# An edge loop of graph attention on Trainium2: another order of VectorE's work, with the running maximum ahead of the merge

## The chip, the cores and the metric

The kernel runs on one core of one Trainium2 chip, which has eight. The metric is the device time of one execution in microseconds, the median of several. Its engines: TensorE (PE, with its weight loads as PEld), VectorE (DVE), ScalarE (ACT), GpSimd (POOL) and SyncE (SP); the last two here mostly issue transfers, which 16 DMA engines carry out.

## The reference

One layer for 1250 nodes of 512 features and 20000 edges that are sorted by their target node:

```
xn = layernorm(x)
r  = [xn[src], xn[dst], edge] @ Wr.T + br ;  k = r @ Wk.T + bk ;  v = r @ Wv.T + bv      # 8 heads of 64
a  = sum over a head of q[dst] * k, times 1/8
attn = softmax of a over the edges of each target ;  out = segment_sum(v * attn, dst) @ Wo.T + bo
x  = x + batchnorm(xn + out) + linear_attention(xn)
x  = x + ffn(layernorm(x))                        # ternary weights, activations rounded to int8
```

The change is in the part from the edge products to the segment sums.

## The kernel before, in words

A prologue folds the weights, so that an edge's key and value are the edge's features times two 512x512 matrices (M) plus a row of a table of the source node, and writes to HBM a table of queries, a table of keys and values, and four empty tables (merge0 to merge3) of merged rows. Then the function `edges` runs over the 20000 edges, in 157 tiles of 128 edges, two tiles to a pair, 79 pairs. After it come the linear attention, the sums over the tables and the feed-forward part.

Products keep float32 precision by splitting each operand into a high part (rounded to fp32r, made by ScalarE) and a low part (the rest, made by VectorE). For a pair p:

- SyncE loads dst_line and end_line (lines 1099 and 1101, target and run-end indices broadcast to all partitions), cut_line (1105) and the edge features efT (1096, 512 KB a pair). Its queue works in order; dst_line of a pair waits for the one-hots of the pair two before, cut_line for a scan (line 1104), and the next efT is issued behind that.
- GpSimd issues indirect transfers, one for each tile: the queries q (qc), the older merged rows (old) and the keys and values of the source (kv), line 1111, and it stores merged rows into a table (merge<-new, line 1140).
- TensorE: `keys` and `values` (24 matmuls a tile, 128x512, lines 1401 to 1405), `sort_scores` (1428, 1429) brings the scores into an order by runs of equal target, `turn_runs` (1437) transposes their running maximum, `spread_top` (1446, 1447) takes each edge's run maximum to its row, and `sums` (1462 to 1465) adds the exponentials and weighted values of equal targets.
- VectorE: `add_k`, `times_q`, `sum_scores` (1255, 1264, 1273) and `add_v` (1307) use the products; `row_one_hots` (1242, 1246), `rank_one_hots` (1234) make the matrices of the sums; `scan` (1322) is the running maximum; `maximum` (1331, 1336, 1338) takes the maximum with the older row of the target and the differences for the exponential; `exp_low_part` (1298), `wv_low_part` (1314), `runs_low_part` (1290), `low_part` (1227) are low parts; `scale_den` (1346) and `merge_rows` (1355, 1357) add the sums to the older rows.
- ScalarE: `high_part` (1166), `copy_runs` (1173), `weights` (1182 exponential, 1184 its high part), `weigh_v` (1193 eight heads, 1198 high part), `scale_old` (1205).

All engines loop over p from 0 to 80, each with an order written out by hand, and wait for each other's semaphores. Each works in its order alone: an instruction that waits holds up all that stand behind it. In turn p, TensorE makes the keys and values of pair p, the run maxima of pair p - 1 and the sums of pair p - 2; VectorE merges pair p - 2 and takes the maximum of pair p - 1. GpSimd's order in a turn is

```
fetch_q(p + 1) ; fetch_old(p - 1) ; fetch_kv(p + 1) ; store(p - 2)
```

where the store waits for the end of `merge_rows(p - 2)` (line 1136). A fetch of older rows waits for the store of the pair two before into the same table (line 1132), and `maximum` waits for the landing of the fetched rows (line 1328). `sort_scores(p)` on TensorE waits for the merge of pair p - 2 (line 1427).

Of the kernel before, what the change touches and what calls it, by code (L numbers as in the profile page):

```python
# [50 lines left out]
def tiles_of(p):  # L51
    return 2 if 2 * p + 1 < ET else 1
# [932 lines left out]
def edges(nc, ef, q_table, kv_table, merge, ident, Me_hi, Me_lo, dst_rows, end_rows, cut_rows, src_id, dst_id, put_id,  # L985
          dst_f, rank, iota_row, iota_col, xT_hi, xT_lo, xnT):

    with ExitStack() as ctx:
# [54 lines left out]
        def landed(p):  # L1043

            return 16 * sum(tiles_of(k) for k in range(p % 2, p + 1, 2))
# [19 lines left out]
        def newmax_at(p):  # L1065

            return 3 * p + 1

        def diff_at(p):
            return 3 * p + 3  # L1070

        def scaled_at(p):

            return 2 * p + 1
# [4 lines left out]
        def exp_at(p):  # L1079

            return 2 * p + 1

        def exp_hi_at(p):
            return 2 * p + 2
# [74 lines left out]
        @block.scalar  # L1159
        def _(act):  # L1160
            def high_part(p):
                b, n = p % 2, tiles_of(p)
                act.wait_ge(ef_in[b], 16 * (p // 2 + 1))
                if p >= 2:
                    act.wait_ge(v_done, 2 * (p - 1))
                act.activation(efT_hi[b][:, 0:n, :, :], efT[b][:, 0:n, :, :], ACT.Copy).then_inc(hi_ready, 1)  # L1166

            def copy_runs(p):
                n = tiles_of(p)
                act.wait_ge(runs_turned, 2 * p + n)  # L1170
                if p >= 1:
                    act.wait_ge(top_done, 2 * p)
                act.activation(runs_hi[:, 0:n, :], turned_s[:, 0:n, :], ACT.Copy).then_inc(runs_copied, 1)

            def weights(p):
                n = tiles_of(p)
                act.wait_ge(max_step, diff_at(p))
                if p >= 2:
                    act.wait_ge(summed, 2 * (p - 1))
                    act.wait_ge(den_step, scaled_at(p - 2))  # L1180
                    act.wait_ge(exp_low, p - 1)
                act.activation(expd[p % 2][:, 0:n, :, :], diff[p % 2][:, 0:n, :, :], ACT.Exp, scale=SCALE).then_inc(exp_ready, 1)  # L1182
                act.wait_ge(exp_ready, exp_at(p))
                act.activation(exp_hi[p % 2][:, 0:n, :], expd[p % 2][:, 0:n, 0, :], ACT.Copy).then_inc(exp_ready, 1)

            def weigh_v(t):
                p, u = t // 2, t % 2
                act.wait_ge(exp_ready, exp_at(p))
                act.wait_ge(v_added, t + 1)
                if p >= 1:  # L1190
                    act.wait_ge(wv_lo_ready, t - 1)
                for h in range(H):
                    act.activation(wv[:, u, h * DH:(h + 1) * DH], vv[p % 2][:, u, h * DH:(h + 1) * DH], ACT.Copy,  # L1193
                                   scale=expd[p % 2][:, u, 0, h:h + 1]).then_inc(wv_ready, 1)
                act.wait_ge(wv_ready, H * (t + 1))
                if p >= 1:
                    act.wait_ge(summed, t - 1)
                act.activation(wv_hi[:, u, :], wv[:, u, :], ACT.Copy).then_inc(wv_hi_ready, 1)  # L1198

            def scale_old(p):  # L1200
                for u in range(tiles_of(p)):
                    act.wait_ge(old_in[p % 2], landed(p))
                    for h in range(H):
                        rows = old[p % 2][:, u, h * DH:(h + 1) * DH]
                        act.activation(rows, rows, ACT.Copy, scale=expd[p % 2][:, u, 1, h:h + 1]).then_inc(old_scaled, 1)  # L1205

            high_part(0)
            for p in range(PAIRS + 2):
                if p >= 2 and tiles_of(p - 2) == 2:
                    weigh_v(2 * p - 3)  # L1210
                if p + 1 < PAIRS:
                    high_part(p + 1)
                if p >= 2:
                    scale_old(p - 2)
                if 1 <= p <= PAIRS:
                    copy_runs(p - 1)
                    weights(p - 1)
                    weigh_v(2 * p - 2)

        @block.vector  # L1220
        def _(dve):
            def low_part(p):
                b, n = p % 2, tiles_of(p)
                dve.wait_ge(hi_ready, p + 1)
                if p >= 2:
                    dve.wait_ge(v_done, 2 * (p - 1))
                dve.tensor_tensor(efT_lo[b][:, 0:n, :, :], efT[b][:, 0:n, :, :], efT_hi[b][:, 0:n, :, :].bitcast(F32),
                                  ALU.subtract).then_inc(lo_ready, 1)
# [64 lines left out]
            def exp_low_part(p):  # L1293
                b, n = p % 2, tiles_of(p)
                dve.wait_ge(exp_ready, exp_hi_at(p))
                if p >= 2:
                    dve.wait_ge(summed, 2 * (p - 1))
                dve.tensor_tensor(exp_lo[b][:, 0:n, :], expd[b][:, 0:n, 0, :], exp_hi[b][:, 0:n, :].bitcast(F32),
                                  ALU.subtract).then_inc(exp_low, 1)

            def add_v(t):
                p, u = t // 2, t % 2
                dve.wait_ge(v_done, t + 1)
                dve.wait_ge(kv_in[p % 2], landed(p))
                if p >= 2:
                    dve.wait_ge(wv_ready, H * (t - 3))
                dve.tensor_tensor(vv[p % 2][:, u, :], psV[u][:, :], kv[p % 2][:, u, D:2 * D], ALU.add).then_inc(v_added, 1)

            def wv_low_part(t):
                u = t % 2  # L1310
                dve.wait_ge(wv_hi_ready, t + 1)
                if t >= 2:
                    dve.wait_ge(summed, t - 1)
                dve.tensor_tensor(wv_lo[:, u, :], wv[:, u, :], wv_hi[:, u, :].bitcast(F32), ALU.subtract).then_inc(wv_lo_ready, 1)  # L1314
# [10 lines left out]
            def maximum(p):  # L1325
                b, n = p % 2, tiles_of(p)
                dve.wait_ge(top_done, 2 * p + n)
                dve.wait_ge(old_in[b], landed(p))
                if p >= 2:
                    dve.wait_ge(put[b], landed(p - 2))  # L1330
                dve.tensor_tensor(new[b][:, 0:n, ROW:TROW], old[b][:, 0:n, ROW:TROW], top[:, 0:n, :],
                                  ALU.max).then_inc(max_step, 1)
                dve.wait_ge(max_step, newmax_at(p))
                if p >= 2:
                    dve.wait_ge(exp_ready, exp_at(p - 2))
                dve.tensor_tensor(diff[b][:, 0:n, 0, :], score[b][:, 0:n, :], new[b][:, 0:n, ROW:TROW],
                                  ALU.subtract).then_inc(max_step, 1)
                dve.tensor_tensor(diff[b][:, 0:n, 1, :], old[b][:, 0:n, ROW:TROW], new[b][:, 0:n, ROW:TROW],  # L1338
                                  ALU.subtract).then_inc(max_step, 1)
# [22 lines left out]
            for p in range(PAIRS + 2):  # L1362
                here, last, older = p < PAIRS, 1 <= p <= PAIRS, p >= 2
                if last:
                    add_v(2 * p - 2)
                if older:
                    exp_low_part(p - 2)
                    wv_low_part(2 * p - 4)
                if last and tiles_of(p - 1) == 2:
                    add_v(2 * p - 1)  # L1370
                if last:
                    row_one_hots(p - 1)
                    scan(p - 1)
                if older and tiles_of(p - 2) == 2:
                    wv_low_part(2 * p - 3)
                if here:
                    for t in range(2 * p, 2 * p + tiles_of(p)):
                        add_k(t)
                        times_q(t)
                        sum_scores(t)  # L1380
                if last:
                    runs_low_part(p - 1)
                if here:
                    split_scores(p)
                    rank_one_hots(p)
                if p + 1 < PAIRS:
                    low_part(p + 1)
                if older:
                    scale_den(p - 2)
                    merge_rows(p - 2)  # L1390
                if last:
                    maximum(p - 1)
            for c in range(C):
                dve.tensor_tensor(xnT[:, c, :], xT_hi[:, c, :].bitcast(F32), xT_lo[:, c, :].bitcast(F32), ALU.add)

# [450 lines left out]
```

## Time and profile before

| | us |
|---|---|
| median of 3 runs | 1852.33 |
| lowest and highest | 1850.69, 1859.62 |
| the profiled execution, its own time | 1861.11 |
| its span | 1859.4 |
| busy: TensorE | 1625.0 (87%) |
| busy: VectorE | 1301.8 (70%) |
| busy: ScalarE | 1026.1 (55%) |
| busy: GpSimd | 698.6 (38%) |
| first and last sort_scores seen in the edge loop | 296.86, 1405.44 |

The span is from the first to the last instruction that the profile records; the run's own time has 1.7 us more. The edge loop takes some 1110 us of it, about 280 us of prologue stand before it and 450 us of other stages behind it. The granted clock of TensorE was 0.938 of full speed over the span, and 1.00 in the windows of the edge loop from 300 to 1300 us. Times in rows are microseconds from the span's start, and a busy time can overlap another on TensorE, whose matmuls are pipelined. A line number is that of the kernel printed above.

### The profile page before, as it was taken

The numbers are of one execution on the slowest core, as the hardware profiler recorded it, in microseconds if no ns is written. First come the engines' busy times: TensorE is split into PE (matmuls) and PEld (weight loads), VectorE is DVE, ScalarE is ACT, GpSimd is POOL, SyncE is SP. The second block draws the span as 40 slices with busy tenths as digits, with TensorE's granted clock in tenths as the row PEclk, the third lists the DMA queues.
The fourth block names the chain that finished last, engine by engine and source line by source line (L and its number), as shares of the span: only waits on it lengthen the run. The fifth ranks groups of instructions, "written<-read, shape, count | busy, mean of one in ns | idle before, by whom it ended". The sixth has DMA issues, their size and how long they took to land. (4 is left out here: it accounts for less than half of the span.)

```text
span 1859.4 us, 26827 instructions
## 1 busy us (share of the span) xinstructions
PE 1625.0 (87%) x7160; PEld 1189.9 (64%) x7162; DVE 1301.8 (70%) x3259; ACT 1026.1 (55%) x3674; POOL 698.6 (38%) x723
## 2 busy tenths in 40 slices
PE   7989979999999999999999999999992777888523
PEld 6867767777777777777777777777772333444311
DVE  5875728788877888778878788788774445332688
ACT  3982225777677776777677776777664334200011
POOL 0001224555555555555555555555542000000033
PEclk9989989999999999999999999999996788999855
DMA  5664327566656666566665666566652433000001
GB/s 179 204 224 157 123 87 229 190 203 205 220 196 191 207 209 220 192 198 206 220 207 193 207 211 223 195 208 208 203 181 101 142 102 136 0 1 1 23 12 44
DMA packets 129671, 300.29 MB, mean 162 GB/s; under 512 B 29088, under 2 KB 50727, under 8 KB 129522
## 3 DMA queue, kind: packets, MB, share of 16 engines
q0 software_dynamic: 63600, 180.17, 28.7%
q1 hardware_dynamic: 60738, 107.59, 18.7%
q10 hardware_dynamic: 5184, 10.81, 1.5%
q8 instruction: 61, 1.00, 0.2%
q14 instruction: 88, 0.72, 0.1%
HBM read 271.40 MB, written 66.58 MB: 182 GB/s over the span
## 5 line engine op out<-in xcount | busy, mean ns | idle before, releaser
L1193 ACT ACTIVATE wv<-vv,expd 128x64 f32<-128x64 f32 x1256 | 315.2, 333 | 0.0
L1205 ACT ACTIVATE old<-old,expd 128x64 f32<-128x64 f32 x1256 | 307.8, 333 | 0.0
L1140 POOL DMA_INDIRECT merge<-new,put_id x157 | 159.9, 1019 | 374.5 <-DVE new L1357 341.3
L1401 PE MATMUL psK<-M_hi,efT_hi 128*128 128x512 f32 x628 | 253.2, 403 | 6.3 <-ACT efT_hi L1166 6.3
L1401 PE MATMUL psV<-M_hi,efT_hi 128*128 128x512 f32 x628 | 255.8, 407 | 0.0
L1402 PE MATMUL psK<-M_lo,efT_hi 128*128 128x512 f32 x628 | 249.5, 397 | 0.0
L1402 PE MATMUL psV<-M_lo,efT_hi 128*128 128x512 f32 x628 | 249.5, 397 | 0.0
L1314 DVE TENSOR_TENSOR wv_lo<-wv,wv_hi 128x512 fp32r<-128x512 f32 x157 | 108.9, 693 | 196.2 <-ACT wv_hi L1198 190.5
L1111 POOL DMA_INDIRECT kv<-kv_table,src_id x157 | 164.3, 1047 | 74.9 <-issue 30.8
L1182 ACT ACTIVATE expd<-diff 128x32 f32<-128x32 f32 (+1 forms) x79 | 18.1, 229 | 310.4 <-DVE diff L1338 310.4
L1111 POOL DMA_INDIRECT qc<-q_table,dst_id x157 | 155.4, 990 | 53.7 <-issue 46.9
L1405 PE MATMUL psK<-M_hi,efT_lo 128*128 128x512 f32 x628 | 172.8, 397 | 0.0
L1405 PE MATMUL psV<-M_hi,efT_lo 128*128 128x512 f32 x628 | 172.4, 396 | 0.0
L1111 POOL DMA_INDIRECT old<-merge,dst_id x157 | 151.4, 965 | 50.5 <-issue 46.7
L1401 PEld LDWEIGHTS psK<-M_hi,efT_hi 128*128 128x128 f32 x628 | 118.6, 189 | 31.5 <-ACT efT_hi L1166 6.7
L1405 PEld LDWEIGHTS psK<-M_hi,efT_lo 128*128 128x128 f32 x628 | 118.4, 189 | 28.9
L1405 PEld LDWEIGHTS psV<-M_hi,efT_lo 128*128 128x128 f32 x628 | 118.3, 188 | 29.0
L1402 PEld LDWEIGHTS psK<-M_lo,efT_hi 128*128 128x128 f32 x628 | 118.9, 189 | 25.9
L1402 PEld LDWEIGHTS psV<-M_lo,efT_hi 128*128 128x128 f32 x628 | 118.9, 189 | 25.5
L1401 PEld LDWEIGHTS psV<-M_hi,efT_hi 128*128 128x128 f32 x628 | 118.7, 189 | 24.9
L1636 POOL MEMSET onem<- 128x128 f32 x1 | 0.2, 204 | 324.2 <-POOLq L1487 324.2
L1264 DVE TENSOR_TENSOR kq<-kk,qc 128x520 f32<-128x520 f32 x157 | 110.1, 701 | 8.1 <-DMA qc<-q_table,dst_id 2.7
(271 smaller groups left out, 3310.1 us busy)
## 6 DMA issues: line engine op xcount, KB each, us to landing
efT<-in_ef_turned_dram SPq DMA_DIRECT2D x78, 512.0 KB, 6.7
merge<-empty ACTq DMA_DIRECT2D x4, 2640.0 KB, 9.7
rows<-merge SPq DMA_DIRECT2D x40, 264.0 KB, 3.5
row_block<-dst_rows POOLq DMA_DIRECT2D x13, 768.0 KB, 5.9
dst_line<-dst_rows SPq DMA_DIRECT2D x78, 128.0 KB, 3.5
end_line<-end_rows SPq DMA_DIRECT2D x78, 128.0 KB, 5.3
kv_table<-kv_out SPq DMA_DIRECT2D x10, 512.0 KB, 3.3
raw<-in_L_gnn_Wr_dram SPq DMA_DIRECT2D x12, 256.0 KB, 5.4
```

Of the source, the lines that this page charges most:

```text
L1111: pool.indirect_dma_start(out=out, out_offset=None, in_=table[:, :], in_offset=bass.IndirectOffsetOnAxis(ap=ids[:, t:t + 1], axis=0)).then ...
L1140: pool.indirect_dma_start(out=merge[2 * (p % 2) + u][:, :], out_offset=bass.IndirectOffsetOnAxis(ap=put_id[:, t:t + 1], axis=0), in_=new[p ...
L1182: act.activation(expd[p % 2][:, 0:n, :, :], diff[p % 2][:, 0:n, :, :], ACT.Exp, scale=SCALE).then_inc(exp_ready, 1)
L1193: act.activation(wv[:, u, h * DH:(h + 1) * DH], vv[p % 2][:, u, h * DH:(h + 1) * DH], ACT.Copy, scale=expd[p % 2][:, u, 0, h:h + 1]).then_ ...
L1205: act.activation(rows, rows, ACT.Copy, scale=expd[p % 2][:, u, 1, h:h + 1]).then_inc(old_scaled, 1)
L1264: dve.tensor_tensor(kq[:, u, :, :].rearrange("p h e -> p (h e)"), kk[:, u, :, :].rearrange("p h e -> p (h e)"), qc[p % 2][:, u, :], ALU.mu ...
L1314: dve.tensor_tensor(wv_lo[:, u, :], wv[:, u, :], wv_hi[:, u, :].bitcast(F32), ALU.subtract).then_inc(wv_lo_ready, 1)
L1401: pe.matmul(out[:, :], efT_hi[b][:, u, c, :], Me_hi[:, c, col:col + D], start=c == 0, stop=False)
L1402: pe.matmul(out[:, :], efT_hi[b][:, u, c, :], Me_lo[:, c, col:col + D], start=False, stop=False)
L1405: last = pe.matmul(out[:, :], efT_lo[b][:, u, c, :], Me_hi[:, c, col:col + D], start=False, stop=c == C - 1)
L1636: pool.memset(onem[:, :], 1.0).then_inc(cst, 1)
```

## The change

Three moves in VectorE's loop and one in ScalarE's; no operation is added or removed.

- `exp_low_part(p - 2)` and both `wv_low_part` of pair p - 2 now stand behind `row_one_hots(p - 1)` and `scan(p - 1)`; before, the first of them stood between the two `add_v` and the second behind the scan.
- `maximum(p - 1)` now stands ahead of `scale_den(p - 2)` and `merge_rows(p - 2)`; before, behind them.
- The exponentials' high part (line 1184) becomes `weights_high`, issued behind the first `weigh_v` of the pair instead of ahead of it.

```diff
@@ ScalarE
                 act.activation(expd[p % 2][:, 0:n, :, :], diff[p % 2][:, 0:n, :, :], ACT.Exp, scale=SCALE).then_inc(exp_ready, 1)
+
+            def weights_high(p):
+                n = tiles_of(p)
                 act.wait_ge(exp_ready, exp_at(p))
                 act.activation(exp_hi[p % 2][:, 0:n, :], expd[p % 2][:, 0:n, 0, :], ACT.Copy).then_inc(exp_ready, 1)
...
                     weights(p - 1)
                     weigh_v(2 * p - 2)
+                    weights_high(p - 1)
@@ VectorE
                 if last:
                     add_v(2 * p - 2)
-                if older:
-                    exp_low_part(p - 2)
-                    wv_low_part(2 * p - 4)
                 if last and tiles_of(p - 1) == 2:
                     add_v(2 * p - 1)
                 if last:
                     row_one_hots(p - 1)
                     scan(p - 1)
-                if older and tiles_of(p - 2) == 2:
-                    wv_low_part(2 * p - 3)
+                if older:
+                    exp_low_part(p - 2)
+                    for t in range(2 * p - 4, 2 * p - 4 + tiles_of(p - 2)):
+                        wv_low_part(t)
                 if here:
                     for t in range(2 * p, 2 * p + tiles_of(p)):
                         add_k(t)
...
                 if p + 1 < PAIRS:
                     low_part(p + 1)
+                if last:
+                    maximum(p - 1)
                 if older:
                     scale_den(p - 2)
                     merge_rows(p - 2)
-                if last:
-                    maximum(p - 1)
```

## Rows read from the trace of the kernel before

**Rows 1.** Stretch, busy us (instructions) of PE, PEld, DVE, ACT, POOL; granted clock, DMA share, GB/s.
```profile
400.00:1300.00 900.00, 876.17 (x4125) 680.55 (x4123) 723.25 (x1626) 650.53 (x2382) 503.86 (x502) 1.00 0.63 206
```

**Rows 2.** Instructions on the older rows' tile, 400 to 1300 us: starts; issue to landing.
```profile
L1331 DVE TENSOR_TENSOR new<-old,psT x62: 153/167/173, 410.4 to 1288.9; 128x16 f32<-128x16 f32 x62
...
DMA to landing us min/median/max: 5.2/6.6/8.8
```

**Rows 3.** TensorE's order in time, early in the loop: start, duration, line.
```profile
296.86 0.22 PE L1428 MATMUL psO<-to_rank,score_hi 128*8 128x128 f32 x1
...
310.59 0.22 PE L1428 MATMUL psO<-to_rank,score_hi 128*8 128x128 f32 x1
```

**Rows 4.** TensorE's order in time in a steady turn.
```profile
822.15 0.28 PE L1437 MATMUL psT<-ident,runs 8*128 8x8 f32 x2
...
825.73 1.09 PE L1405 MATMUL psV<-M_hi,efT_lo 128*128 128x512 f32 x4
827.05 0.24 PE L1446 MATMUL psT<-runs_hi,from_end 128*128 128x8 f32 x1 [0.23 <-issue]
```

**Rows 5.** VectorE's order in time, the same turn; idle time before in brackets.
```profile
801.56 0.17 DVE L1331 TENSOR_TENSOR new<-old,psT 128x16 f32<-128x16 f32 x1 [1.37 <-issue]
...
814.42 0.17 DVE L1346 TENSOR_TENSOR old_den<-old,expd 128x16 f32<-128x16 f32 x1
...
815.70 0.16 DVE L1357 TENSOR_TENSOR new<-psO,old_den 128x16 f32<-128x16 f32 x1
815.78 0.16 DVE L1331 TENSOR_TENSOR new<-old,psT 128x16 f32<-128x16 f32 x1
...
816.15 0.68 DVE L1307 TENSOR_TENSOR vv<-psV,kv 128x512 f32<-128x512 f32 x1
...
819.36 0.69 DVE L1314 TENSOR_TENSOR wv_lo<-wv,wv_hi 128x512 fp32r<-128x512 f32 x1 [2.40 <-ACT wv_hi L1198]
...
821.19 0.67 DVE L1322 TENSOR_TENSOR_SCAN runs<-cut_line,psO 8x256 f32<-8x256 f32 x1
...
826.77 0.17 DVE L1290 TENSOR_TENSOR runs_lo<-psT,runs_hi 128x16 fp32r<-128x16 f32 x1
...
828.62 0.17 DVE L1346 TENSOR_TENSOR old_den<-old,expd 128x16 f32<-128x16 f32 x1
```

**Rows 6.** ScalarE's order in time in the same turn.
```profile
821.27 0.63 ACT L1198 ACTIVATE wv_hi<-wv 128x512 fp32r<-128x512 f32 x1
...
826.58 0.16 ACT L1173 ACTIVATE runs_hi<-psT 128x16 fp32r<-128x16 f32 x1
```

**Rows 7.** GpSimd's order in time: a store held up, and the steady turn.
```profile
660.19 1.27 POOL L1140 DMA_INDIRECT merge<-new,put_id  x1 [1.99 <-issue]
...
816.68 1.02 POOL L1140 DMA_INDIRECT merge<-new,put_id  x1 [5.76 <-DVE new L1357]
...
823.16 0.95 POOL L1111 DMA_INDIRECT old<-merge,dst_id  x1 [0.30 <-issue]
```

**Rows 8.** SyncE's order in time in the same two turns.
```profile
663.21 0.33 SPq L1096 DMA_DIRECT2D efT<-in_ef_turned_dram  x1
...
822.57 0.33 SPq L1096 DMA_DIRECT2D efT<-in_ef_turned_dram  x1
```

**Rows 9.** Three single second fetches of older rows, each with its landing time.
```profile
L1111 POOL DMA_INDIRECT old<-merge,dst_id x1: 946/946/946, 665.6 to 665.6; - x1
DMA to landing us min/median/max: 5.3/5.3/5.3
...
L1111 POOL DMA_INDIRECT old<-merge,dst_id x1: 944/944/944, 1025.3 to 1025.3; - x1
DMA to landing us min/median/max: 6.0/6.0/6.0
...
L1111 POOL DMA_INDIRECT old<-merge,dst_id x1: 982/982/982, 1399.3 to 1399.3; - x1
DMA to landing us min/median/max: 3.4/3.4/3.4
```

## The prediction, made before the changed kernel was run

> **What bounds the kernel now.** I began with the table by stretches, to see which engine fills the edge loop, where the change is. In its steady part TensorE is busy 876 of 900 us, VectorE 723 and ScalarE 651 [rows 1]: TensorE is the nearest to full, yet it loses 24 us there. One pair of edge tiles is one turn of all the engines' loops; the steady turn is (1288.9 - 410.4) / 61 = 14.40 us, by the 62 maxima of line 1331 [rows 2].
>
> Next, the order in time on TensorE. In the first pairs of the loop, before any merged row holds anyone up, a turn from L1428 to L1428 is 310.59 - 296.86 = 13.73 us [rows 3]. In the steady part the last value product ends its issue at about 825.73 + 4 x 0.234 = 826.67 and spread_top starts at 827.05, 0.38 us late [rows 4]. So TensorE could turn in 13.73, and something else holds it to 14.2 and, in bad turns, to more.
>
> That something is on VectorE and ScalarE. From one maximum (801.56) to the next (815.78), in a turn where the second waited for nothing, is 14.22 us [rows 5]. The chain: differences, exponentials, both weighted values with the second high part ending at 821.27 + 0.63 = 821.90 [rows 6], its low part, keys and scores, runs_lo behind ScalarE's copy of 826.58, low part of the edges, merge, maximum. It holds 2.40 us in which VectorE waits at the first wv_lo, with the scan queued behind it. The maximum at 801.56 had itself waited 1.37 us [rows 5]: for no engine, so for a transfer.
>
> The last view is GpSimd's and the transfers'. The end of a merge (815.70 + 0.16 = 815.86) lets the store go at 816.68; two stores, two fetches of q and two of the older rows follow, the last at 823.16 [rows 5, 7]. The old rows land 5.2 to 8.8 us after their issue, half of them by 6.6 [rows 2]; the second of a pair, which counts, is mostly near 6.8. From merge to landing: 0.82 + 6.48 + 6.8 + 0.1 allowed for the signal = 14.2 us. So a second loop, merge, store, fetch, maximum, is as long as a turn; today it is open, since the maximum stands behind the merge of its iteration and can be late without delaying that store.
>
> **The change, part by part.** No instruction is added or taken away, and no transfer; all is order. M is the start of a maximum, and the rows of 815.78 serve for a turn.
>
> Maximum in front of the merge. The chain through ScalarE loses scale_den and merge, 814.42 to 815.86 = 1.44 us [rows 5]. Its length becomes: wv_hi of the second tile at M+6.12, wv_lo and keys and scores to M+11.0, runs_lo at M+11.1 (ScalarE's copy starts at 826.58 - 815.78 = 10.8), then the 1.85 us to 828.62 with which a merge began before [rows 5, 6]: 13.0 us. That is under 13.73, so this chain ceases to bind. The 0.38 us before spread_top goes, since the copy comes earlier against TensorE's order.
>
> The price: the merge stands 0.37 us later behind the maximum (three small operations, 815.78 to 816.15 [rows 5]), and it is now behind the maximum's wait for the old rows. Queued behind that wait are scale_den, both merges, the store, and behind the store on GpSimd's queue all fetches of q, old rows and kv; TensorE's sort_scores also waits for the merge. The second loop closes: 0.37 + 1.44 + 0.82 + 6.48 + 0.1 + L = 9.2 + L, L being the landing time of the second old fetch. With L = 6.8 it would be 16.0 us a turn; TensorE's 13.73 needs L of 4.5.
>
> Values, one-hots and scan in front of the low parts. Their own length is unchanged, and what was the wait of 2.40 us shrinks, as the second wait for wv_hi falls after the scan. The scan's end was 821.19 + 0.67, M+6.1; it now has the merge of 1.44 us ahead of it, and no longer the wait of 2.40 and the 0.7 us of exp_low and wv_lo: about M+4.4 [rows 5]. turn_runs at 822.15 [rows 4] then has ample time, also in the turns in which it was late before. Both wv_lo still end at M+6.8, where sums needs the second one at about M+8. Should TensorE reach it earlier, sums would wait by the difference. The moved scan and one-hots also release SyncE's queue: dst_line and end_line, then cut_line and efT. The efT load of 512 KB was issued at 822.57, 0.6 us ahead of the second old fetch [rows 7, 8]; it will go at about M+5.1, 4.0 us ahead of M+9.1. So 512 KB and the lines leave the time of the old fetches and meet those of q.
>
> What is L then? No row has this distance. The nearest: a turn in which a store was held up, so that the old fetch went at 665.62 and efT at 663.21, 2.4 us ahead; its L is 5.3, and a second such turn has 6.0 [rows 7, 8, 9]. At the other end an old pair with nothing beside it, and no q ahead of it, has 3.4 [rows 9]. A line through 0.6 us and 6.8, and 2.4 us and 5.65 (the mean of the two) falls by 0.63 us for each us; at 4.0 us it gives 4.65. I take 4.7, since the two rows with contention are the nearer ones and it is the line's value; ends 3.4 and 6.0 stay for the range. For L alone the Trainium skill's page "DMA: Bandwidth & Descriptors", section "Anatomy of one DMA — SWDGE (gpsimd) path", has about 2.0 us and the bytes at 436 GB/s; for 270 KB that is an estimate of 2.6 us, by which the loop would be 11.8 us and TensorE would bind. The trace speaks against it: 3.4 us alone, 6.6 in company [rows 2, 9].
>
> Exponentials' high part behind the first weighted value. It frees ScalarE by 0.1 us at the start and is due at the low part, M+4.4 at the earliest, and done by about M+3.6. Nothing, and without that 0.8 us cover still hidden by the wait for wv_hi at M+6.1.
>
> The sum: 9.2 + 4.7 = 13.9 us. To it come 0.15 for scatter, as a turn can't fall under 13.73 but can go over, and 0.05 for held stores: 14.1 us. Over 74 turns (79 pairs less start and drain) (14.1 - 14.4) x 74 = -22 us. Against the profiled execution's own 1861.1 us that is 1839; it stands 8.8 us above the median of 1852.3, so 1830 for the median. Beyond 0.5% (9 us) a measurement can tell it from no change; 9 us is 0.12 us a turn.
>
> **The rivals.** (a) TensorE binds all through: L under 4.4, a turn of 13.75, -48 us, 1804. For it: an old fetch alone has 3.4. Against it: two q fetches stand in the same queue just ahead. Chance 0.12.
>
> (b) No difference: L of 4.95 to 5.25, a turn within 0.12 of 14.4: 1843 to 1861. The gain of the shorter chain is given back to the closed loop. Chance 0.17.
>
> (c) Slower. Place: the wait of line 1331 for the old rows, with merge and store behind it. It decides from L of 5.3: each us above goes wholly into the turn. If the early efT load helps no more than in the two held turns, L = 5.65, a turn 9.2 + 5.65 + 0.05 = 14.9, +37 us, 1889. For it: these are the only rows measured. Against it: there efT still went only 2.4 us ahead. Chance 0.21.
>
> (d) The same mechanism in full: L stays 6.8, 16.0 a turn, +118 us, 1971. Mechanism: what is drawn from two queues in turns has to be served before the last old row either way, and taking efT earlier only moves its share to the q fetches, which hold up the old ones behind them. That L was 5.3 and 6.0 in the held turns speaks against it. Chance 0.05. The Trainium skill, "DMA: Bandwidth & Descriptors", section "Queues, rings and completion order", says that each DMA engine goes round-robin between the queues that have work; the overlap itself agrees with it, the fall in L less so.
>
> **How the numbers follow.** The forecast, L of 4.4 to 4.95, 1808 to 1843, has 0.45. Faster: 0.45 + 0.12 = 0.57, less the edge of the forecast's own band, 0.55. Same 0.17 and that edge, 0.19. Slower 0.21 + 0.05 = 0.26. The range goes from 1802, the floor of case (a), to 1886, inside case (c); outside lie (d) and the worse half of (c), with a little below.
>
> **What would show it.** L1331's idle, in most turns none before, grows to several tenths of a us a turn, and PE's wait goes from L1446 to L1428, behind L1357. SyncE issues efT before the first q fetch. The second old fetch lands in 4.7 us. The idle before L1314 shrinks from 2.4 to about 1 us, that before L1437 vanishes. If L is above 5.3 I am wrong in sign; if L1331 doesn't wait at all, in size. Wrong too if VectorE's turn isn't 13.0, seen as waits at L1446 that remain.

## The result, and the profile after

| | us |
|---|---|
| before, median of 4 runs | 1855.97 |
| after, median of 4 runs | 1919.63 (1915.48 to 1924.18) |
| ratio after to before | 1.034, 95% interval 1.029 to 1.039 |
| span of the profiled execution after | 1920.5 |

The change makes the kernel 3.4% slower; 1830 was forecast, with 1886 as the upper end. Each group of runs below timed the kernel before as well, and in two of them it took 2027 to 2048 us instead of 1850 to 1864, while the changed kernel, run in one of the two, took its usual time; ratios from those groups are not used, only their times.

First the same table by stretches as in [rows 1], for the changed kernel:

```profile
400.00:1300.00 900.00, 832.13 (x3885) 648.78 (x3886) 676.48 (x1530) 611.59 (x2241) 529.10 (x471) 0.99 0.61 194
```

TensorE is busy 832 us of 900, not 876: it stands 68 us where it stood 24, at nearly the same clock. A turn, from one maximum to the next, has a mean of 15.29 us over the 58 that the trace shows in this stretch, against 14.40. Over 74 turns that is 0.89 x 74 = 66 us, and the result is 64 us. From the first to the last sort_scores of the loop (the trace's first is at 284.5, not at 296.86 as the table above has it) the time goes from 1121 to 1186 us: the whole loss is in the edge loop.

Now the waits in the same stretch (engine, line, who released it; us in total, times, longest):

```profile
POOL merge L1140 <- DVE new L1361: 159.2, 58, 4.1
DVE new L1335 <- issue: 124.0, 53, 3.5
POOL old L1111 <- DMA merge<-new,put_id: 98.3, 59, 3.1
...
DVE wv_lo L1318 <- ACT wv_hi L1201: 74.5, 59, 1.3
PE psO L1431 <- DVE new L1361: 67.4, 55, 2.3
```

Line 1335 is the maximum (1331 before). It waits in 53 turns, 124 us together, and no engine releases it: it waits for the older rows. In the trace it starts 0.08 us (median) behind the landing of the second fetch. TensorE's sort_scores waits behind it for the merge. The wait at wv_lo fell from 2.4 to 1.3 us a turn, as the change wanted. New is the third row: GpSimd's fetch of older rows waits for the landing of the merged rows' store, in every turn. That wait was absent before in this stretch.

One turn in order of time, VectorE first; these lines answer to [rows 5]:

```profile
812.13 0.17 DVE L1335 TENSOR_TENSOR new<-old,psT 128x16 f32<-128x16 f32 x1 [3.38 <-issue]
...
813.80 0.16 DVE L1361 TENSOR_TENSOR new<-psO,old_den 128x16 f32<-128x16 f32 x1
...
815.67 0.67 DVE L1326 TENSOR_TENSOR_SCAN runs<-cut_line,psO 8x256 f32<-8x256 f32 x1
...
827.35 0.17 DVE L1335 TENSOR_TENSOR new<-old,psT 128x16 f32<-128x16 f32 x1 [1.42 <-PE psT L1450]
```

Then GpSimd in the same turn, which answers to [rows 7]:

```profile
814.77 1.02 POOL L1140 DMA_INDIRECT merge<-new,put_id  x1 [2.70 <-DVE new L1361]
816.10 1.79 POOL L1140 DMA_INDIRECT merge<-new,put_id  x1 [0.30 <-issue]
818.19 0.99 POOL L1111 DMA_INDIRECT qc<-q_table,dst_id  x1 [0.30 <-issue]
819.49 0.98 POOL L1111 DMA_INDIRECT qc<-q_table,dst_id  x1 [0.30 <-issue]
822.43 0.95 POOL L1111 DMA_INDIRECT old<-merge,dst_id  x1 [1.96 <-DMA merge<-new,put_id]
823.69 0.94 POOL L1111 DMA_INDIRECT old<-merge,dst_id  x1 [0.30 <-issue]
```

And SyncE, which answers to [rows 8]:

```profile
815.78 0.32 SPq L1099 DMA_DIRECT2D dst_line<-dst_rows  x1
...
817.04 0.33 SPq L1096 DMA_DIRECT2D efT<-in_ef_turned_dram  x1
```

From the first maximum to the second: 1.83 us to the end of the merge (813.96), 0.81 to the first store, 1.33 to the second, 6.33 to the first old fetch, 1.26 to the second, and from there 3.66 to the next maximum. Sum 15.22 us. The profile puts this one wait down to TensorE's psT, but the last record of that ends at 826.8; the fetch landed after 3.6 us, at 827.3, and is what ended the wait. Over all turns of the stretch the means are 1.83, 0.82, 8.84 (the three parts from the first store to the second fetch) and 3.78 us, 15.3 together. The loop merge, store, fetch, maximum closed as the prediction said, but with other parts. The landing times of the two stores of this turn and of its second old fetch:

```profile
L1140 POOL DMA_INDIRECT merge<-new,put_id x1: 1018/1018/1018, 814.8 to 814.8; - x1
DMA to landing us min/median/max: 2.2/2.2/2.2
...
L1140 POOL DMA_INDIRECT merge<-new,put_id x1: 1792/1792/1792, 816.1 to 816.1; - x1
DMA to landing us min/median/max: 6.1/6.1/6.1
...
L1111 POOL DMA_INDIRECT old<-merge,dst_id x1: 944/944/944, 823.7 to 823.7; - x1
DMA to landing us min/median/max: 3.6/3.6/3.6
```

The second store lands 6.1 us after its issue. All stores of the kernel before, 400 to 1300 us:

```profile
DMA to landing us min/median/max: 2.2/2.3/3.5
```

The old fetch behind it lands in 3.6 us, where the one of [rows 7] took 7.0.

What the transfers did meanwhile is in the packets. From 817.0 to 820.0 us, within the 6.1 us of the second store, those of SyncE's queue (q1) alone ran (packets, MB, share of the 16 engines); GpSimd's queue had none:

```profile
q1 hardware_dynamic: 339, 0.49, 67.0%
```

The second store's own packets ran from 820.3 to 821.2. In the mean of the stretch they begin 4.2 us behind the issue, with some 390 packets of SyncE's queue ahead of them; in the kernel before they begin after 1.6 us with none ahead.

### The profile page after: what moved, and what is told of

Read it like the earlier page. It is cut to its first block and busy times, and to the rows that moved or that the text cites. A ratio compares the mean times of both kernels' runs of the same rounds, so it can differ in the third digit from the quotient of the medians.

```text
span 1920.5 us, 26829 instructions
## 1 busy us (share of the span) xinstructions
PE 1633.4 (85%) x7162; PEld 1197.2 (62%) x7162; DVE 1295.7 (67%) x3259; ACT 1026.4 (53%) x3674; POOL 772.1 (40%) x723
## 5 line engine op out<-in xcount | busy, mean ns | idle before, releaser
L1140 POOL DMA_INDIRECT merge<-new,put_id x157 | 215.8, 1374 | 259.5 <-DVE new L1361 227.7
L1404 PE MATMUL psK<-M_hi,efT_hi 128*128 128x512 f32 x628 | 258.5, 412 | 6.3 <-ACT efT_hi L1166 6.3
L1111 POOL DMA_INDIRECT old<-merge,dst_id x157 | 171.2, 1090 | 156.7 <-DMA merge<-new,put_id 131.8
L1335 DVE TENSOR_TENSOR new<-old,psT 128x16 f32<-128x16 f32 (+1 forms) x79 | 13.5, 171 | 175.0 <-issue 163.4
```

The costliest lines, as they stand in the source:

```text
L1111: pool.indirect_dma_start(out=out, out_offset=None, in_=table[:, :], in_offset=bass.IndirectOffsetOnAxis(ap=ids[:, t:t + 1], axis=0)).then ...
L1140: pool.indirect_dma_start(out=merge[2 * (p % 2) + u][:, :], out_offset=bass.IndirectOffsetOnAxis(ap=put_id[:, t:t + 1], axis=0), in_=new[p ...
L1404: pe.matmul(out[:, :], efT_hi[b][:, u, c, :], Me_hi[:, c, col:col + D], start=c == 0, stop=False)
```

## The experiments

**Theory 1**: what costs is the closed loop, long here because the second store lands late, and that because the moved scan releases SyncE's loads at the time of the stores. **Theory 2**: the store is slow because VectorE works beside it where it idled before. **Theory 3**: the early scan alone costs, the closed loop nothing. **Theory 4**: the moved maximum costs by something else than the loop. Turns, landings and waits below are of the stretch from 400 to 1300 us unless another is named.

**One part at a time.** `max_only` is the kernel before with this edit alone:

```diff
+                if last:
+                    maximum(p - 1)
                 if older:
                     scale_den(p - 2)
                     merge_rows(p - 2)
-                if last:
-                    maximum(p - 1)
```

> The kernel before with the maximum alone moved ahead of the merge; low parts, scan and exponentials as before. Theory 1: the loop through the stores is closed, but SyncE's loads come behind the stores: the second store lands in 2.3 us, the older rows, with edge features 2 us ahead, in 5.3 to 6 us, a turn of 14.6 to 15.2 us, 1870 to 1915 us. Theory 3 (closing the loop costs nothing, only the early scan does): a turn of at most 14.2 us, 1840 us or less.

Measured: 1934.82 us, ratio 1.0425 (1.040 to 1.045). The maximum alone is slower than the whole change. The mean turn is 15.35 us, and the maximum waits in all 59 turns. From its waits:

```profile
DVE new L1331 <- issue: 123.9, 53, 4.1
...
POOL old L1111 <- DMA merge<-new,put_id: 1.9, 2, 1.0
```

The landing of its stores:

```profile
DMA to landing us min/median/max: 2.2/2.4/4.2
```

The stores land in 2.4 us and the old fetch hardly waits for them. The second old fetches are issued 6.75 us after the first store and land in 5.85 us, in the mean: 1.83 + 0.82 + 6.75 + 5.85 + 0.1 = 15.35 us. Theory 3 falls. My own number, 1915 at most, was 20 us too low.

`scan_only` is the changed kernel with that edit undone; the early one-hots and scan and the late high part stay.

> The changed kernel with the maximum put back behind the merge: values, one-hots and scan ahead of the low parts and the late high part remain. Theory 1: the second store still lands late (4 to 6 us, loads at its side) and the old fetch waits for it, but the loop is open and the older rows land ahead of their maximum: no wait at the maximum, the turn is VectorE's and ScalarE's chain of 14.2 us, 1838 to 1852 us. Theory 3: the early scan alone makes it slower, a turn above 14.8 us, 1885 us or more.

Measured: 1847.56 us, ratio 0.9954 (0.9937 to 0.9971), half a per cent faster than the kernel before. The maximum never waits; the turn is 14.29 us. The landing of the older rows:

```profile
DMA to landing us min/median/max: 3.2/3.7/4.5
```

and, in its waits, that of their fetch for the stores, and one for the late high part:

```profile
POOL old L1111 <- DMA merge<-new,put_id: 86.4, 61, 3.1
...
DVE exp_lo L1302 <- ACT exp_hi L1187: 39.5, 63, 0.7
```

The late store is here too: the second lands in 4.8 us in the mean (5.8 in the changed kernel), the fetch waits 1.4 us a turn for it (1.7), and that costs nothing, since nothing that waits for the old rows holds up the next store.

**The loop closed without moving anything.** `closed_by_wait` is the kernel before with one wait for the same landing, ahead of the merge:

```diff
                 if older:
+                    if p - 1 < PAIRS:
+                        dve.wait_ge(old_in[(p - 1) % 2], landed(p - 1))
                     scale_den(p - 2)
```

> The kernel before, its order untouched, with one wait added on VectorE ahead of the merge: for the landing of the older rows for which the maximum behind the merge waits anyway. Theory 1 (it is the merge behind that landing, not the order as such, that costs): the loop merge, store, old fetch, landing is closed as in the changed kernel, 1.44 + 0.8 + 6.6 + 0.1 us and a landing of 5.9 to 6.8 us, 14.8 to 15.7 us a turn, 1885 to 1960 us. Theory 4 (another effect of the moved maximum): within 10 us of the kernel before.

Measured: 1946.84 us, ratio 1.0501 (1.048 to 1.052), the slowest of the kernels made here. The wait is now in front of scale_den, in all 58 turns that the trace shows:

```profile
DVE old_den L1346 <- DMA old<-merge,dst_id: 69.2, 58, 1.9
```

The turn is 15.51 us in the mean. The second old fetch is issued 6.54 us after the first store and lands in 6.67: 1.44 + 0.82 + 6.54 + 6.67 + 0.1 = 15.57. This is the clearest of the runs: with every instruction in its old place, the wait alone costs 93 us. Theory 4 falls. TensorE's sort_scores waits for the late merge as well, here and in max_only (69.0 us); `max_old_first_timed` below keeps the merge behind the maximum, and there that wait is 6.2 us.

**The loads moved away.** `before_late_loads` and `after_late_loads` are the two kernels with SyncE held back:

```diff
                 if p >= 2:
                     sp.wait_ge(onehots, 3 * (p - 1))
+                    sp.wait_ge(score_step, 4 * p)
```

> The kernel before with the same holding back of SyncE's loads. Theory 1: the older rows land in 3.5 to 4.5 us instead of 6.8, the maximum never waits for them, and what remains is the chain of 14.2 us: 1838 to 1850 us, 5 to 15 us under the kernel before. If loads late in the turn hurt by themselves (edge features late for ScalarE's high part), over 1860 us.

Measured: 1846.44 us, ratio 0.9947 (0.9925 to 0.9969); turn 14.26 us, no wait at the maximum. As theory 1 says, most of what the kernel before lost above 14.2 us a turn it lost to old rows that came late beside the loads: 8.3 us of waits at its maximum in this stretch, of some 12 us over 61 turns.

> The changed kernel, with SyncE's lines and edge features of the next pairs held back until the second tile's scores are summed (about 11 us after the maximum). Theory 1 (the closed loop merge, store, landing of the store, old fetch, maximum is long because the second store lands in 5.6 us instead of 2.3, and it does so because the moved scan releases SyncE's loads at the moment of the stores): the second store lands in 2.3 to 3 us again, the old fetch stops waiting for it, lands in 3.5 to 4.5 us, the turn falls from 15.3 to 13.8 to 14.1 us and the kernel to 1815 to 1835 us, faster than both. Theory 2 (the second store is slow because VectorE is at work beside it where it idled before; the loads are not to blame): the second store keeps its 1.8 us duration and a landing above 4.5 us, the turn stays above 15 us, 1905 to 1925 us.

Measured: 1877.57 us (1859.3 to 1897.8), ratio 1.0152 (1.009 to 1.021). The profiled execution is the fastest of its four, 1859.3 us, with a turn of 14.41. From 600 to 1000 us the second store lands in 3.7 us in the mean, against 5.7 in the changed kernel, while its own duration stays long, 1.5 us against 1.75. So the loads make most of the late landing, as theory 1 has it; in scan_only, with the loads and a duration of 1.0, it lands in 4.7. The longer issue has a smaller share: in after_late_loads the store's packets begin 2.2 us behind it, against 1.6 in the kernel before and 4.2 in the changed one. Why the issue itself takes longer, VectorE's work beside it or another cause, no run shows. My time was 40 us too low. What is late next, in its waits:

```profile
DVE new L1336 <- issue: 36.0, 26, 3.4
...
ACT efT_hi L1167 <- DMA efT<-in_ef_turned_dram: 29.7, 35, 2.1
DVE kk L1260 <- DMA kv<-kv_table,src_id: 28.0, 39, 1.7
```

The edge features now come late for ScalarE and the source rows late for VectorE, and both stores land in 3.7 us, as they meet the tail of the loads. Why its other executions took 1877 us and more no profile shows.

**The two fetches of q taken out of the loop.** On GpSimd the old fetches go first, in five kernels. The first, `max_only_old_first`, is max_only with this edit:

```diff
-                if p + 1 < PAIRS:
-                    fetch_q(p + 1)
                 if 1 <= p <= PAIRS:
                     fetch_old(p - 1)
                 if p + 1 < PAIRS:
+                    fetch_q(p + 1)
                     fetch_kv(p + 1)
```

> The kernel with the maximum alone moved, and on GpSimd the fetches of older rows taken ahead of those of q. Theory 1 (what makes the moved maximum slow is the loop merge, store, old fetch, landing, maximum): two fetches of q, 2.6 us of issue, leave the loop, the old fetch then waits for the store's landing (2.4 us) and is issued about 5.1 us behind the first store instead of 6.7; with a landing of 5 to 6 us the loop is 12.9 to 13.9 us and TensorE's 13.75 binds. 13.8 to 14.1 us a turn, 1815 to 1840 us, against 1935 without the reordering. Theory 4 (the moved maximum costs by something else, such as the merge 0.4 us later for TensorE): it stays near 1935 us.

It took 1852.44 us, beside a kernel before of 2033, so no ratio can be taken from it. The same kernel stands twice more below, as `max_only_old_first_again` and `max_old_first_timed`.

> The same kernel as max_only_old_first, since the kernel before took 2033 us beside it where it takes 1855 us elsewhere. Theory 1: beside a kernel before of about 1855 us it takes 1825 to 1845 us; beside one of 2033 us again some 1852 us, as its loop tolerates slower transfers. If its first result came from the chip alone it is within 1% of the kernel before.

Again 1852.11, and the kernel before 2042.

> The moved maximum with the old fetches first, once more beside the kernel before, for a ratio where the kernel before takes about 1855 us: 0.992 to 1.002.

Measured: 1823.95 us (1819.8 to 1831.3), beside a kernel before of 1854.07: ratio 0.9842 (0.982 to 0.987). It is faster than both kernels, and than expected. Its table by stretches and its waits:

```profile
400.00:1300.00 900.00, 893.02 (x4259) 707.13 (x4259) 750.19 (x1678) 666.43 (x2443) 561.44 (x517) 1.00 0.67 213
```

```profile
POOL old L1111 <- DMA merge<-new,put_id: 161.8, 64, 4.1
...
DVE new L1330 <- PE psT L1446: 28.4, 41, 1.8
DVE new L1330 <- issue: 18.3, 15, 2.3
```

TensorE is busy 893 of 900 us, the median turn is 13.75 us (the mean 13.98), near the 13.73 of [rows 3] as TensorE's own, and where the maximum waits it is mostly for TensorE. Half of the older rows land by 4.4 us. In max_only the same order of VectorE cost 4.3%; with the fetches of q out of the loop it gains 1.6%. Little of the gain is the 2.6 us of their issue: the old fetch now waits 2.5 us a turn for the stores instead, and from the first store to the second old fetch it is 6.4 us in the mean, against 6.75. The larger part is the landing of the second old fetch, 4.5 us against 5.85.

`after_old_first` is the changed kernel with the old fetches first.

> The changed kernel with the same reordering on GpSimd. Theory 1: here the old fetch already waits for the landing of the second store, 5.6 us behind its issue, with both fetches of q issued within that time, so it can't go earlier; only their traffic leaves its way. The turn falls by 0.3 us at most from 15.3, 1895 to 1915 us. If the reordering helps as much as with the maximum alone (turn under 14.3 us, under 1850 us), the landing of the store isn't what holds the changed kernel.

Measured: 1944.88 us, beside a kernel before of 2033, and 20 us above the 1925 that the changed kernel took in the next group. The expectation missed on the slow side. Its first wait is

```profile
POOL old L1111 <- DMA merge<-new,put_id: 250.2, 57, 5.9
```

4.4 us a turn instead of 1.7. Before, the two fetches of q were issued in the shadow of the store's landing; now they and kv stand behind it. The queue has 2.6 us of stores, 4.4 of waiting and 7.7 of fetches, 14.7 us, and some of its issues last longer than the 0.95 us of before, beside a turn of 15.53: GpSimd's queue is nearly full, and its stores hardly wait for VectorE.

`scan_only_old_first` is scan_only with the old fetches first.

> The changed kernel with the maximum behind the merge again, and the old fetches first. The loop is open and the older rows already landed ahead of the maximum without this. Theory 1: no change against 1847.6 us, the chain of 14.2 us binds: 1842 to 1853 us. Theory 4: if GpSimd's order matters by itself, outside of that.

Measured: 1924.09 us, 64 us above scan_only, which took 1859.92 in the next group; expected was no change. The wait for the store is 270.6 us in 59 turns, 4.6 each, and the same sum, 2.6 + 4.6 + 7.7 = 14.9, stands beside a turn of 15.35. So the order that helps where the stores land in 2.4 to 3.5 us seems to cost where the second lands late, with an open loop too. How much it costs isn't settled: both kernels ran only beside a kernel before of 2033, and in their profiles VectorE also waits 17 to 24 us for signals that come late (last section), which no profile of the other groups shows.

`after_old_first_mid` is after_old_first ("the same" is that kernel) with `sp.wait_ge(k_added, 2 * p)` where before_late_loads has its line.

> The same, and SyncE's loads held back until the second tile's keys are added, some 9 us after the maximum, behind the issue of the old fetch. Theory 1: the second store lands in 2.3 to 3.5 us again, the old fetch follows it at once, lands in 3.5 to 5 us, the loop is 11.5 to 13.5 us, TensorE binds at 13.75 to 14.1 us: 1812 to 1840 us. Theory 2 (VectorE's work beside the store, not the loads): landing above 4.5 us, turn above 14.5 us, over 1870 us.

Measured: 1890.02 us, 55 us less than after_old_first, 50 us more than expected: the direction of theory 1, not its size. This profile too has VectorE waiting for late signals, 35 us.

`max_old_first_mid` is max_old_first_timed with that same line on SyncE.

> The same with SyncE's loads held back until the second tile's keys are added, behind the issue of the old fetch. Theory 1: the older rows land in 4 to 5 us instead of 6, the stores in 2.3 to 3.7, the loop is under 13.5 us and TensorE binds at 13.75 to 13.95 us: 1815 to 1832 us. If stores or edge features then land too late, 1840 us or more with waits at efT_hi.

Measured: 1855.3 us, ratio 1.001 (0.9994 to 1.0026), 31 us slower than without the holding back. The second fetch of older rows landed in 4.4 us in the mean, within what was expected but no sooner than without (4.5); the old fetch still waited for the stores, 167.1 us in all, and VectorE waited 32.1 us for kv instead of 16.2. The loads moved away from the old rows come in the way of others.

**The kernels once more, side by side.** The changed kernel, scan_only and the kernel before, in the second of the groups with a slow kernel before:

> The changed kernel itself beside the others of this call. Theory 1: 1910 to 1930 us where the kernel before takes about 1855 us, the second store landing in 5 to 6 us; if the transfers are slower here, both are slower, and the difference shows whether the closed loop suffers more.

1925.46 us, 6 us off its first result.

> Maximum behind the merge, the early scan kept. 1842 to 1853 us beside a kernel before of 1855 us, as measured; beside one of 2033 us clearly under it, as the older rows land some 2 us sooner with the loads ahead of them.

1859.92 us (1852.8 to 1875.7).

> The kernel before with a profile from the same chip: landing of the older rows near 6.8 us and turns of 14.4 us if it takes about 1855 us; if it takes about 2030 us, the theory says that its maximum waits for the older rows in every turn, about 2 us, with landings above 9 us, since its own loop merge, store, fetch, maximum then binds too.

2038.64 us, but not as expected: its maximum waits hardly at all. What it shows stands in the last section.

## Why the prediction was wrong

It was wrong in sign: 1830 us forecast, 1920 measured, above the range's end of 1886; a slower kernel had a chance of 0.26.

The steps that held: that the wait of the maximum for the older rows would hold up merge and store and so close a second loop (closed_by_wait and max_only show it apart); that ScalarE's chain would fall below TensorE's 13.73 (max_old_first_timed has a median turn of 13.75, and the waits ahead of spread_top are gone from it and from the changed kernel); the scan's end at about M+4.4 (816.34 - 812.13 = 4.2) and the edge features' issue at M+5.1 (817.04, M+4.9); that old rows land sooner with the loads ahead of them. The landing even fell further than forecast, to a mean of 3.7 us for the second fetch, against 4.7. How much of that came of the error below isn't known: by it the fetch went 6.5 us behind the edge features' load in the mean and not 4.0, but in scan_only, at 5.1 us, it lands in 3.7 as well.

The step that failed is a term of the sum, "0.37 + 1.44 + 0.82 + 6.48 + 0.1 + L". The 6.48 us from the first store to the second old fetch were taken from a turn with no loads at the stores' side, and kept. There they were only GpSimd's issue. In the turn shown of the changed kernel they are 1.33 + 6.33 + 1.26 = 8.92 us (8.84 in the mean), since the fetch waits for the second store to land (line 1132), and that takes 5.7 us instead of 2.5 in the mean from 600 to 1000 us. The wait for the store was in the code and in its description above; the prediction asked whom the early loads would leave alone, the old fetches, and named q as the only ones that they meet. They meet the stores first: dst_line was issued at 815.78, the second store at 816.10. With the measured parts the sum closes: 1.83 + 0.81 + 8.92 + 3.66 = 15.22 us. A late store isn't the only way to such a loop: in max_only the stores land in 2.4 us, the second fetch of older rows in 5.85, and the loop is as long.

Rival (c) named the right place, the maximum's wait with merge and store behind it, but its price of 1889 hung on L alone, and by L alone the kernel would have been faster. Rival (d), the full 6.8 us, didn't happen for the old rows; what it says of traffic that only moves is what happened to the stores. Taking turns is not how it looks, though: from 817.0 to 820.0 us 339 packets of the loads' queue ran and none of GpSimd's, and then the store's ran. The page "DMA: Bandwidth & Descriptors" of the Trainium skill, section "Queues, rings and completion order", cited there, says that each DMA engine goes round-robin between the queues that have work. This turn shows no such turn-taking; whether GpSimd's queue had work ready in these 3 us no row shows, so why the store's packets began so late stays open.

The late high part was priced at nothing, hidden by the wait for wv_hi. No run has it alone. In scan_only VectorE waits 0.6 us a turn for it (39.5 us in 63 turns), and at wv_lo 1.8 us instead of the 2.4 of before, the same sum, which agrees.

## What to carry to other kernels

Before a wait is moved ahead of other work, follow what stands behind it round to its own cause: here maximum, merge, store, fetch, landing, maximum. While one link is behind the wait in the queue, the loop is open and its length costs nothing; closed, every part of it counts once a turn, and it has to be shorter than the turn of the engine that bounds the kernel. Transfers that are moved go into someone else's time, so list each transfer of the turn, the small stores first, with who waits for its landing; and shorten a loop before closing it (the same moved maximum was 4.3% slower with the fetches of q inside the loop and 1.6% faster with them outside).

## What was not expected of the hardware

A store of merged rows is small. In the trace of the kernel before, 400 to 1300 us, GpSimd's queue has 1078 packets of 2116 bytes, the size of one row (2112 bytes) and 4 more, for 124 stores: some 9 rows or 18 KB each, by an estimate that counts every such packet as a row of a store. Yet one took 6.1 us to land beside a load of 512 KB and two broadcast lines of 128 KB, where half of the stores before took 2.3 or less. Its size doesn't tell its time.

The kernel before took 2027 to 2048 us in all its runs of two groups, and 1850 to 1864 in the rest. In the profile of before_again VectorE waits 34 times in 53 turns for a key product that TensorE's records show as ended:

```profile
809.68 1.10 PE L1405 MATMUL psK<-M_hi,efT_lo 128*128 128x512 f32 x4
```

```profile
813.80 0.69 DVE L1255 TENSOR_TENSOR kk<-psK,kv 128x512 f32<-128x512 f32 x1 [3.56 <-remote]
```

The product is over by 810.8, its reader starts at 813.80, and ScalarE's runs_hi, which waits for TensorE's next result, at 813.87. Turns of 17.8 us follow, and the clock granted to TensorE is 0.92 of full from 400 to 600 us, where it was 1.00 in that stretch of the first profile. Neither changed_again, scan_only_again nor max_only_old_first_again, of the same group, has such turns. But six of the seven other profiles of these two groups have a few such waits, 3 to 15 each, and no profile of the other groups has any from 400 to 1300 us. In max_only_old_first they stand mostly at the maximum:

```profile
DVE new L1330 <- remote: 16.0, 9, 1.9
```

All such waits are 19 and 23 us of the 900 in that kernel's two profiles here, where it took 28 us more than in max_old_first_timed. What holds the signals isn't settled.
